# Non-local attention block: g projected by channels in two column halves and turned by transposes, second output projection one slot later

## The chip, the cores and the metric

One core of a Trainium2 chip runs the whole kernel. The metric is the device time of one execution in microseconds (us). Three executions of the kernel before took 215.80, 217.01 and 214.25 us, median 215.8. A fourth execution was profiled; it took 214.18 us.

## The reference

For each of 8 images, x is 128 channels by 1024 pixels (f32). Three 1x1 convolutions give theta and phi (64 channels each) and g (64 channels):

```
g     = w_g x + b_g          theta = w_theta x + b_theta      phi = w_phi x + b_phi
att   = softmax over m of (theta_n . phi_m)                   1024 x 1024 per image
y_n   = sum over m of att[n, m] g[m]
out   = x + BN(w_out y + b_out)                               BN: scale and shift by channel
```

The batch norm uses given means and variances, so it is one scale (INV) and one shift (SHIFT) by channel; the bias of g is folded into SHIFT.

## The kernel before

**Tiles.** An image has 8 tiles of 128 rows n of the attention matrix, the 8 images 64 tiles. Four tiles make a half (512 pixels), for which one value sum and one output projection are made. Every engine has its own program, written as a function `step(it, k)`; k counts tiles, and j = k % 8 is called the slot here. `run_steps` unrolls the first and last steps and puts 16 steps (two images) in a loop. The order within an engine is the order written out in `step`; between engines only semaphores order the work.

**A tile's way.** PE makes the scores of tile k+1 in step k (`scores`, L713: theta and phi split into high and low parts, four matmuls of 512 columns). VectorE takes the row maximum (L579), ScalarE the exponential with its row sum (L537), into `probs`. PE then turns the tile ("flips", L778, eight 128x128 transposes into the two banks ps_flip[0] and ps_flip[1]) in step k+2. ScalarE copies the flips as f16 high parts (pt_hi, L525), VectorE computes the f16 low parts (pt_lo, L678). One tile in four (slots 1 and 5) goes another way: GpSimd splits it (p_hi L402, p_lo L406) and the DMA queue transposes it (L296, L305), so steps 3 and 7 have no flips. A flip set may overwrite a bank of ps_flip only when pt_lo of the flip set before has read it (`pt_lo_ready`). The scores of tile k+1 overwrite the bank of tile k-1 and wait for its exponential (`probs_ready`).

**A half's way.** The value sums accumulate in ps_y: `sum_high` (L725, eight matmuls of f16, stationary 128 columns) in slots 3 and 7, `sum_low` (L732, eight matmuls of 64 stationary columns, alternating between the two column halves of the array) in slots 5 and 1. VectorE scales the sum into y_norm in slots 6 and 2 (`scale_y`, L596). PE makes the output projection into the bank ps_misc (`convolve`, L739) in the same slots 6 and 2. VectorE adds it to the residual (`add_residual`, L589) in slots 7 and 3, and SyncE's queue stores it.

**The next image.** PE also computes the projections of image b+1 while image b is worked on, all in the same bank ps_misc: theta/phi in slots 0 and 1 (L803), g in slot 4 (`project_g`, L697: for each of 8 pixel tiles x is the stationary operand and w_g moves, so that pixels come out on partitions). ScalarE copies g to g_raw in slot 5 (`evacuate_g`, L481). VectorE takes the peak of g in slot 6 (`peak_of_g`, L573), PE transposes it over all partitions in slot 7 (`spread_peak`, L719), and VectorE reads it in slot 0 and computes the scale (L647 to L656). GpSimd then makes the f16 parts of g: g_parts high and g_scaled in slot 0, g_parts low in slot 1 (L410 to L419). GpSimd also splits theta/phi (hi in slot 2, lo in slots 3 and 4) and x (x_hi, x_lo in slots 5 and 7), and writes the residual's start (resid, L448, slot 1). The high and low parts of theta/phi are restacked by six DMAs per image (L286); the scores of the next image's first tile, made in slot 7, wait for all of them (`stacked`).

**The DMA queue.** SyncE issues in one order per image (`image`, L327): inverse sums to DRAM, store of the second half of image b-2 (L283), x loads (L264, waiting for resid), transpose of p_hi, broadcast of inverse sums, transpose of p_lo, restacks of hi, store, inverse sums, restacks of lo, broadcast, transposes.

## Time and profile before

| | |
|---|---|
| median of three runs | 215.8 us (214.25 to 217.01) |
| the profiled execution's own time | 214.18 us |
| its span, first to last instruction | 212.4 us |
| PE busy | 202.0 us (95%) |
| VectorE (DVE) busy | 181.7 us (86%) |
| ScalarE (ACT) busy | 143.4 us (68%) |
| GpSimd (POOL) busy | 130.6 us (61%) |
| mean granted TensorE clock | 1.000 |
| share of PE in the chain that ended last | 61% |

The page gives one profiled execution. Busy shares say how full an engine is, not whether the end waits for it. The chain of waits goes back from the last instruction to what released each step; the timeline gives the start and length of each instruction in order, with the releaser of idle time in square brackets. In rows of PE, "x8" counts recorded matmuls; an f32 matmul that isn't a transpose is recorded as two. The span leaves out what lies around the instructions, here 1.8 us.

### The profile page before, as it was taken

What the parts mean: (1) busy time and instruction counts of PE and PEld (TensorE: products, weight loads), DVE (VectorE), ACT (ScalarE), POOL (GpSimd) and SP (SyncE); (2) the same over time, 40 slices, a digit from 0 to 9 for tenths busy, and PEclk for the clock granted to TensorE, in tenths of its full rate; (3) what the DMA queues carried; (4) which work ended last, traced back from release to release, by engine and by line L of the source; (5) the groups of instructions that cost most, each with busy time, mean ns of one, the idle gap of its engine ahead of it and who ended that gap; (6) DMA issues with size and microseconds to landing.
All of it is one profiled execution on the core that took longest, in us unless ns stands there. A gap on an engine that the chain in (4) does not pass through costs nothing.

```text
span 212.4 us, 4045 instructions
## 1 busy us (share of the span) xinstructions
PE 202.0 (95%) x1156; PEld 137.4 (65%) x1156; DVE 181.7 (86%) x298; ACT 143.4 (68%) x259; POOL 130.6 (61%) x113
## 2 busy tenths in 40 slices
PE   7997969999999999999999999999999999999994
PEld 6685838576665857577575956668575855656542
DVE  0689987987999799977999599977999789989871
ACT  2777857668585848866596666856696585758721
POOL 2449786848489494866679494885769352913400
PEclk9999999999999999999999999999999999999999
DMA  5225991699529974599819994299924994182102
GB/s 159 83 76 109 210 225 27 174 221 238 114 78 241 245 182 99 126 209 250 158 50 218 243 217 113 87 223 251 167 63 105 222 235 104 38 195 49 49 11 91
DMA packets 44716, 31.61 MB, mean 149 GB/s; under 512 B 35616, under 2 KB 36128, under 8 KB 44704
## 3 DMA queue, kind: packets, MB, share of 16 engines
q1 hardware_dynamic: 44416, 31.34, 63.7%
q10 hardware_dynamic: 288, 0.14, 0.2%
q8 instruction: 5, 0.08, 0.2%
q14 instruction: 7, 0.06, 0.1%
HBM read 8.36 MB, written 4.23 MB: 59 GB/s over the span
## 4 chain that ended last, share of the span: by engine, by line
PE 61%; DVE 14%; issue 8%; ACT 6%; DMA 4%; SPq 3%; POOL 2%; ACTq 1%; DVEq 0%
PE ps_scores L713 18%; PE ps_flip L778 13%; PE ps_y L725 10%; PE ps_misc L697 5%; DVE pt_lo L678 5%; PE ps_y L732 5%; DVE neg_max L579 5%; PE ps_misc L803 4%; PE ps_misc L739 4%; ACT probs L537 3%; DVE y_norm L596 2%; DMA phi_ll<-lo 2%; DMA vec<-vectors_dram 2%; SPq L286 2%; ACT pt_hi L525 2%
## 5 line engine op out<-in xcount | busy, mean ns | idle before, releaser
L537 ACT ACTIVATE probs<-ps_scores,neg_max 128x1024 f32<-128x1024 f32 x64 | 71.7, 1121 | 22.5 <-DVE neg_max L579 22.4
L579 DVE TENSOR_REDUCE neg_max<-ps_scores 128x1 f32<-128x1024 f32 x64 | 77.8, 1215 | 1.2 <-PE ps_scores L713 1.2
L678 DVE SCALAR_TENSOR_TENSOR pt_lo<-ps_flip,pt_hi 128x512 f16<-128x512 f32 x98 | 62.9, 684 | 15.3 <-ACT pt_hi L525 15.1
L525 ACT ACTIVATE pt_hi<-ps_flip 128x512 f16<-128x512 f32 x98 | 53.4, 597 | 26.5 <-PE ps_flip L778 26.5
L778 PE MATMUL ps_flip<-ident,probs 128*128 128x128 f32 x392 | 52.7, 276 | 1.1 <-DVE pt_lo L678 0.6
L778 PEld LDWEIGHTS ps_flip<-ident,probs 128*128 128x128 f32 x392 | 43.6, 142 | 13.8 <-issue 6.1
L713 PE MATMUL ps_scores<-phi_hh,theta_hl 128*128 128x512 f32 x128 | 45.7, 438 | 3.8 <-DMA phi_ll<-lo 1.8
L713 PE MATMUL ps_scores<-phi_ll,theta_hl 128*128 128x512 f32 x128 | 40.0, 393 | 0.0
L406 POOL TENSOR_TENSOR p_lo<-probs,p_hi 128x1024 f16<-128x1024 f32 x15 | 32.3, 2155 | 2.9 <-POOL p_hi L402 2.3
L725 PE MATMUL ps_y<-pt_hi,g_parts 128*128 128x512 f16 (+1 forms) x128 | 30.0, 377 | 0.0
L713 PEld LDWEIGHTS ps_scores<-phi_hh,theta_hl 128*128 128x128 f32 x128 | 19.3, 190 | 14.9 <-ACT probs L537 12.2
L713 PEld LDWEIGHTS ps_scores<-phi_ll,theta_hl 128*128 128x128 f32 x128 | 24.0, 188 | 5.6
L402 POOL TENSOR_SCALAR p_hi<-probs 128x1024 f16<-128x1024 f32 x15 | 15.7, 1047 | 10.8 <-ACT probs L537 9.8
L725 PEld LDWEIGHTS ps_y<-pt_hi,g_parts 128*128 128x128 f16 x128 | 11.4, 98 | 15.4 <-issue 4.2
L457 POOL TENSOR_SCALAR x_hi<-x_in 128x1024 fp32r<-128x1024 f32 x7 | 7.4, 1055 | 18.5 <-PE ps_misc L697 15.7
L462 POOL TENSOR_TENSOR x_lo<-x_in,x_hi 128x512 fp32r<-128x512 f32 x14 | 17.8, 1278 | 0.8
L432 POOL TENSOR_TENSOR lo<-qk,hi 128x512 fp32r<-128x512 f32 x14 | 17.8, 1294 | 0.8
L410 POOL TENSOR_SCALAR g_parts<-g_raw,g_factor 128x512 f16<-128x512 f32 x7 | 4.9, 694 | 20.5 <-DVE g_factor L654 20.5
L739 PE MATMUL ps_misc<-y_norm,wout 128*128 128x512 f32 x30 | 16.2, 621 | 0.9 <-DVE y_norm L596 0.9
L596 DVE SCALAR_TENSOR_TENSOR y_norm<-ps_y,y_unit,inv_all 128x512 f32<-128x512 f32 x15 | 17.0, 1135 | 0.0
L732 PE MATMUL ps_y<-pt_lo,g_parts 128*64 128x512 f16 (+1 forms) x128 | 16.7, 382 | 0.0
L697 PEld LDWEIGHTS ps_misc<-wg,x_in 128*128 128x128 f32 x112 | 13.6, 191 | 0.6
(80 smaller groups left out, 179.3 us busy)
## 6 DMA issues: line engine op xcount, KB each, us to landing
x_in<-x_in_dram SPq DMA_DIRECT2D x16, 256.0 KB, 3.2
inv_all<-inv_row SPq DMA_DIRECT2D x15, 256.0 KB, 3.7
out_dram<-resid SPq DMA_DIRECT2D x15, 256.0 KB, 3.1
phi_hh<-hi SPq DMA_DIRECT2D x14, 256.0 KB, 4.9
phi_ll<-lo SPq DMA_DIRECT2D x14, 256.0 KB, 4.1
theta_hl<-hi SPq DMA_DIRECT2D x7, 256.0 KB, 4.0
theta_hl<-lo SPq DMA_DIRECT2D x7, 256.0 KB, 3.8
pt_hi<-p_hi SPq DMA_TRANSPOSE x15, 3.6
```

What stands on the lines that cost most here:

```text
L406: nc.gpsimd.tensor_tensor(low[:, :], p[:, :], high[:, :], ALU.subtract).then_inc(p_lo_ready, 1)
L525: nc.scalar.activation(pt_hi[ring][:, c * HALF_TILES:(c + 1) * HALF_TILES, slot * P:(slot + 1) * P], ps_flip[c][:, :].rearrange("p (a n) - ...
L537: nc.scalar.activation(probs[k % PROB_RING][:, :], ps_scores[k % 2][:, :], ACT.Exp, bias=neg_max[:, k % STEPS:k % STEPS + 1], accum_out=ro ...
L579: nc.vector.tensor_reduce(out=top, in_=ps_scores[k % 2][:, :], op=ALU.max, axis=AX.X, negate=True).then_inc(row_max_ready if by_dma(it, k) ...
L596: nc.vector.scalar_tensor_tensor(out=y_norm[:, :].rearrange("c (t p) -> c t p", p=P), in0=ps_y[:, :].rearrange("c (t p) -> c t p", p=P), s ...
L678: nc.vector.scalar_tensor_tensor(out=pt_lo[ring][where], in0=ps_flip[c][:, :].rearrange("p (a n) -> p a n", n=P), scalar=PROB_SCALE, in1=p ...
L697: last = nc.tensor.matmul(target[:, m * CI:(m + 1) * CI], x_in[r][:, m * P:(m + 1) * P], wg[:, :], start=True, stop=True)
L713: last = nc.tensor.matmul(ps_scores[k % 2][:, cc], theta_hl[r][:, cols], phi[:, cc], start=(n == 0), stop=(n == 1))
L725: nc.tensor.matmul(target[:, to], g_parts[r][:, m, :], pt_hi[ring][:, m, cols], start=(m == 0), stop=False, skip_group_check=True)
L732: last = nc.tensor.matmul(target[side * CI:(side + 1) * CI, to], g_parts[r][:, m, 0:CI], pt_lo[ring][:, m, cols], start=False, stop=(m >= ...
L739: nc.tensor.matmul(target, wout[:, 0:C], y_norm[:, cols], start=True, stop=True).then_inc(conv_ready, 1)
L778: last = nc.tensor.transpose(ps_flip[c][:, a * P:(a + 1) * P], probs[(k - 2) % PROB_RING][:, m * P:(m + 1) * P], ident[:, :])
```

## The change

- PE, slot 5: g of the next image is computed with w_g (64 columns) as the stationary operand and x moving, 512 pixels for each of two f32 matmuls; pixels 0 to 511 go to partitions 0 to 63 of ps_misc, pixels 512 to 1023 to partitions 64 to 127. It stands directly behind `sum_low`. The eight matmul pairs of slot 4 are gone.
- ScalarE, slot 6: ps_misc is copied to the new buffer g_channels. PE, slot 6: four 128x128 transposes turn it back into ps_misc. ScalarE, slot 7: g_raw is copied from there, with its pixel tiles reordered.
- The peak of g is taken in slot 0 of the next image (VectorE), spread through ps_y in slot 2 (PE, after y_norm of that slot has been made), read in slot 3 (VectorE). The high-half sums of slot 3 wait for that read. GpSimd's three g_parts operations follow in slot 4. Both halves of lo are made in slot 3.
- The output projection of the second half goes from slot 6 to slot 7 (behind the high-half sums, waiting for the copy of g_raw), its residual addition from slot 7 to slot 0 of the next image. The theta/phi projection of slot 0 waits for that addition.
- x_hi waits for the theta/phi projections in place of the g projection.
- VectorE's program unrolls 16 first steps in place of 8.

```diff
--- before.py
+++ after.py
@@ -102,6 +102,7 @@
         theta_hl = [sbuf(f"theta_hl{i}", [P, N], F32R) for i in range(2)]
         phi_hh = [sbuf(f"phi_hh{i}", [P, N], F32R) for i in range(2)]
         phi_ll = [sbuf(f"phi_ll{i}", [P, N], F32R) for i in range(2)]
+        g_channels = sbuf("g_channels", [P, BANK], F32)
         g_raw = sbuf("g_raw", [P, MT, CI], F32)
         g_scaled = sbuf("g_scaled", [P, MT, CI], F32)
         g_parts = [sbuf(f"g_parts{i}", [P, MT, 2 * CI], F16) for i in range(2)]
@@ -163,6 +164,8 @@
         hi_ready = sem("hi_ready")
         lo_ready = sem("lo_ready")
         g_ready = sem("g_ready")
+        g_channels_out = sem("g_channels_out")
+        g_flipped = sem("g_flipped")
         g_out = sem("g_out")
         g_peak_ready = sem("g_peak_ready")
         g_peak_spread = sem("g_peak_spread")
@@ -405,7 +408,21 @@
                     hold(lo_moved[ring], moved_by(it, k - 1) - MOVED)
                     nc.gpsimd.tensor_tensor(low[:, :], p[:, :], high[:, :],
                                             ALU.subtract).then_inc(p_lo_ready, 1)
-                if j == 0 and exists(b, B) and not is_first(b):
+                if j == 2 and exists(b + 1, B):
+                    hold(proj_out, 2 * b + 2)
+                    if not is_first(b):
+
+                        hold(stacked[r], it * 16 * STACKS + 16 * STACKS * ((k // MT + 1) // 2))
+                    nc.gpsimd.tensor_scalar(out=hi[:, :], in0=qk[:, :], scalar1=1.0, scalar2=0.0,
+                                            op0=ALU.mult, op1=ALU.add).then_inc(hi_ready, 1)
+                if j == 3 and exists(b + 1, B):
+                    hold(hi_ready, b + 1)
+                    for c in range(PER_IMAGE):
+                        cols = slice(c * BANK, (c + 1) * BANK)
+                        nc.gpsimd.tensor_tensor(lo[:, cols], qk[:, cols], hi[:, cols].bitcast(F32),
+                                                ALU.subtract).then_inc(lo_ready, 1)
+
+                if j == 4 and exists(b, B) and not is_first(b):
                     hold(g_factor_ready, b + 1)
                     nc.gpsimd.tensor_scalar(out=g_parts[r][:, :, 0:CI], in0=g_raw[:, :, :],
                                             scalar1=g_factor[:, r:r + 1], scalar2=1.0,
@@ -413,27 +430,13 @@
                     nc.gpsimd.tensor_scalar(out=g_scaled[:, :, :], in0=g_raw[:, :, :],
                                             scalar1=g_factor[:, r:r + 1], scalar2=1.0,
                                             op0=ALU.mult, op1=ALU.mult).then_inc(g_scaled_ready, 1)
-                if j == 1 and exists(b, B) and not is_first(b):
                     hold(g_hi_ready, b + 1)
                     hold(g_scaled_ready, b)
                     nc.gpsimd.tensor_tensor(g_parts[r][:, :, CI:2 * CI], g_scaled[:, :, :],
                                             g_parts[r][:, :, 0:CI], ALU.subtract).then_inc(g_split, 1)
 
-                if j == 2 and exists(b + 1, B):
-                    hold(proj_out, 2 * b + 2)
-                    if not is_first(b):
-
-                        hold(stacked[r], it * 16 * STACKS + 16 * STACKS * ((k // MT + 1) // 2))
-                    nc.gpsimd.tensor_scalar(out=hi[:, :], in0=qk[:, :], scalar1=1.0, scalar2=0.0,
-                                            op0=ALU.mult, op1=ALU.add).then_inc(hi_ready, 1)
-                if j in (3, 4) and exists(b + 1, B):
-                    cols = slice((j - 3) * BANK, (j - 2) * BANK)
-                    hold(hi_ready, b + 1)
-                    nc.gpsimd.tensor_tensor(lo[:, cols], qk[:, cols], hi[:, cols].bitcast(F32),
-                                            ALU.subtract).then_inc(lo_ready, 1)
-
                 if j == 5 and exists(b + 2, B):
-                    hold(g_ready, b + 2)
+                    hold(proj_ready, 2 * b + 2)
                     split_x(it * 16 + 16 * (k // STEPS + 2), r, 0)
                     split_x(b + 2, r, 1)
                 if j == 7 and exists(b + 2, B):
@@ -511,9 +514,13 @@
                     nc.scalar.activation(qk[:, c * BANK:(c + 1) * BANK], ps_misc[:, :], ACT.Identity,
                                          bias=BIAS_TP).then_inc(proj_out, 1)
 
-                if j == 5 and exists(image + 1, B):
+                if j == 6 and exists(image + 1, B):
                     act.wait_ge(g_ready, image + 2)
-                    evacuate_g(image + 1, ps_misc[:, :], g_raw[:, :, :].rearrange("p t c -> p (t c)"))
+                    nc.scalar.activation(g_channels[:, :], ps_misc[:, :], ACT.Copy).then_inc(g_channels_out, 1)
+                if j == 7 and exists(image + 1, B):
+                    act.wait_ge(g_flipped, image + 1)
+                    evacuate_g(image + 1, ps_misc[:, :].rearrange("p (a c i) -> p a c i", c=PER_IMAGE, i=CI),
+                               g_raw[:, :, :].rearrange("p (c a) i -> p a c i", c=PER_IMAGE))
 
                 t = tile_at(it, k - 2)
                 if exists(t, TILES) and not by_dma(it, k - 2):
@@ -630,21 +637,15 @@
                 if tile_is(it, k, TILES + 1):
                     scale_y(HALVES - 2, 0, 1, B - 1, 8 * HALVES)
 
-                h = half_at(it, k - 11)
-                if j % HALF_TILES == 3 and exists(h, HALVES - 2):
-                    ring, part = (k - 11) // MT % 2, (k - 11) // HALF_TILES % PER_IMAGE
-                    dve.wait_ge(resid_ready, image_at(it, k - 11) + 1)
-                    add_residual(h, resid[ring][:, part * BANK:(part + 1) * BANK], ps_misc[:, :])
                 if tile_is(it, k, 1):
                     peak_of_g(0, 0)
-                if j == 6 and exists(image + 1, B):
-                    peak_of_g(image + 1, (k // MT + 1) % 2)
-
-                if j == (2 if is_first(image) else 0) and exists(image, B):
+                if j == 0 and exists(image, B) and not is_first(image):
+                    peak_of_g(image, k // MT % 2)
+
+                if j == (2 if is_first(image) else 3) and exists(image, B):
                     r = k // MT % 2
                     dve.wait_ge(g_peak_spread, image + 1)
-                    spread = ps_y if is_first(image) else ps_misc
-                    nc.vector.tensor_reduce(out=g_peak_all[:, r:r + 1], in_=spread[:, 0:P], op=ALU.max,
+                    nc.vector.tensor_reduce(out=g_peak_all[:, r:r + 1], in_=ps_y[:, 0:P], op=ALU.max,
                                             axis=AX.X).then_inc(g_peak_read, 1)
                     dve.wait_ge(g_peak_read, image + 1)
                     nc.vector.tensor_scalar(out=g_unit[:, r:r + 1], in0=g_peak_all[:, r:r + 1],
@@ -656,6 +657,13 @@
                     nc.vector.tensor_scalar(out=y_unit[:, r:r + 1], in0=g_unit[:, r:r + 1],
                                             scalar1=1.0 / PROB_SCALE, scalar2=None,
                                             op0=ALU.mult).then_inc(y_unit_ready, 1)
+
+                back = 11 if j == 3 else 12
+                h = half_at(it, k - back)
+                if j in (0, 3) and exists(h, HALVES - 2):
+                    ring, part = (k - back) // MT % 2, (k - back) // HALF_TILES % PER_IMAGE
+                    dve.wait_ge(resid_ready, image_at(it, k - back) + 1)
+                    add_residual(h, resid[ring][:, part * BANK:(part + 1) * BANK], ps_misc[:, :])
 
                 if tile_is(it, k, 2):
                     dve.wait_ge(g_factor_ready, 1)
@@ -683,7 +691,7 @@
                 if exists(t, TILES):
                     row_maximum(it, k + 1)
 
-            run_steps(dve, step)
+            run_steps(dve, step, head=STEPS)
             dve.wait_ge(resid_ready, B)
             add_residual(HALVES - 2, resid[1][:, 0:BANK], ps_misc[:, :])
             add_residual(HALVES - 1, resid[1][:, BANK:N - P], ps_scores[1][:, 0:BANK - P])
@@ -793,8 +801,7 @@
                         if isinstance(image, int) and image == 0:
                             pe.wait_ge(w_lo_ready, 1)
                         pe.wait_ge(x_lo_ready, 2 * image + 1)
-                        if not is_first(image):
-                            pe.wait_ge(g_peak_read, image + 1)
+                        wait(pe, result_ready, 2 * image - 2)
                     else:
                         pe.wait_ge(x_lo_ready, 2 * image + 2)
                         pe.wait_ge(proj_out, 2 * image + 1)
@@ -804,18 +811,22 @@
                                                 start=(n == 0), stop=(n == 2))
                     last.then_inc(proj_ready, 1)
                 h = half_at(it, k - 10)
-                if j % HALF_TILES == 2 and exists(h, HALVES - 2):
+                if j == 2 and exists(image, B) and not is_first(image):
+                    pe.wait_ge(y_scaled, 2 * image - 1)
+                    spread_peak(image, k // MT % 2, ps_y[:, 0:P])
+                if j == 2 and exists(h, HALVES - 2):
                     if more:
-                        pe.wait_ge(*((proj_out, 2 * image + 2) if j == 2 else (g_out, image + 2)))
+                        pe.wait_ge(proj_out, 2 * image + 2)
                     else:
                         wait(pe, result_ready, h)
                     convolve(h, ps_misc[:, :], slice(0, BANK))
 
-                if j == 4 and more:
-                    pe.wait_ge(proj_out, 2 * image + 2)
-                    wait(pe, result_ready, 2 * image - 1)
-                    project_g(ps_misc, (k // MT + 1) % 2, range(MT)).then_inc(g_ready, 1)
-
+                if j == 6 and more:
+                    pe.wait_ge(g_channels_out, image + 1)
+                    for a in range(HALF_TILES):
+                        last = nc.tensor.transpose(ps_misc[:, a * P:(a + 1) * P],
+                                                   g_channels[:, a * P:(a + 1) * P], ident[:, :])
+                    last.then_inc(g_flipped, 1)
 
                 h, quarter = half_at(it, k - 6), (k - 6) % HALF_TILES
                 if exists(h, HALVES - 2):
@@ -825,6 +836,8 @@
                         pe.wait_ge(hi_moved[ring], moved_by(it, k - 6))
                         pe.wait_ge(g_split, image_at(it, k - 6) + 1)
                         wait(pe, y_scaled, h)
+                        if j == 3:
+                            pe.wait_ge(g_peak_read, image_at(it, k) + 1)
                         sum_high(ring, r, ps_y, slice(0, BANK), slice(0, BANK))
                     if quarter == 3:
                         pe.wait_ge(lo_moved[ring], moved_by(it, k - 6))
@@ -832,9 +845,22 @@
 
                 if tile_is(it, k, 1):
                     spread_peak(0, 0, ps_y[:, 0:P])
-                if j == 7 and more:
-                    wait(pe, result_ready, 2 * image)
-                    spread_peak(image + 1, (k // MT + 1) % 2, ps_misc[:, 0:P])
+                if j == 5 and more:
+                    pe.wait_ge(proj_out, 2 * image + 2)
+                    wait(pe, result_ready, 2 * image - 1)
+                    for c in range(PER_IMAGE):
+                        last = nc.tensor.matmul(ps_misc[c * CI:(c + 1) * CI, :], wg[:, :],
+                                                x_in[(k // MT + 1) % 2][:, c * BANK:(c + 1) * BANK],
+                                                start=True, stop=True, skip_group_check=True)
+                    last.then_inc(g_ready, 1)
+
+                h = half_at(it, k - 11)
+                if j == 7 and exists(h, HALVES - 2):
+                    if more:
+                        pe.wait_ge(g_out, image + 2)
+                    else:
+                        wait(pe, result_ready, h)
+                    convolve(h, ps_misc[:, :], slice(0, BANK))
 
                 if tile_is(it, k, TILES - 1):
                     pe.wait_ge(pt_lo_ready, 2 * flip_at(0, LAST_HALF))
```

## Rows read from the trace of the kernel before

**Rows 1.** The page's first part, busy time of each engine.

```profile
PE 202.0 (95%) x1156; PEld 137.4 (65%) x1156; DVE 181.7 (86%) x298; ACT 143.4 (68%) x259; POOL 130.6 (61%) x113
```

**Rows 2.** Windows view, images 1 to 5: length, then busy us of PE, PEld, DVE, ACT, POOL.

```profile
34.36:155.65 121.29, 120.60 (x697) 82.23 (x696) 109.15 (x176) 85.30 (x156) 84.72 (x70) 1.00 0.74 171
```

**Rows 3.** The chain of waits, in image 2: start us, us, engine and tile.

```profile
61.71 0.98 PE ps_y L732 x8
...
64.65 0.86 PE ps_misc L739 x2
...
66.73 1.74 PE ps_y L725 x8
```

**Rows 4.** Timeline of all engines, PE's rows: start us, us, engine, line, operation.

```profile
141.46 1.04 PE L778 MATMUL ps_flip<-ident,probs 128*128 128x128 f32 x8
...
143.26 1.89 PE L697 MATMUL ps_misc<-wg,x_in 128*128 128x64 f32 x16
...
144.99 1.04 PE L778 MATMUL ps_flip<-ident,probs 128*128 128x128 f32 x8
...
146.89 1.05 PE L732 MATMUL ps_y<-pt_lo,g_parts 128*64 128x512 f16 x8
...
147.87 1.09 PE L778 MATMUL ps_flip<-ident,probs 128*128 128x128 f32 x8
...
149.90 1.13 PE L739 MATMUL ps_misc<-y_norm,wout 128*128 128x512 f32 x2
...
150.80 0.73 PE L713 MATMUL ps_scores<-phi_hh,theta_hl 128*128 128x512 f32 x2
...
151.84 1.90 PE L725 MATMUL ps_y<-pt_hi,g_parts 128*128 128x512 f16 x8
...
153.69 1.04 PE L778 MATMUL ps_flip<-ident,probs 128*128 128x128 f32 x8
```

**Rows 5.** The same timeline, three rows of ACT.

```profile
145.27 0.60 ACT L481 ACTIVATE g_raw<-ps_misc 128x512 f32<-128x512 f32 x1 [0.99 <-PE ps_misc L697]
...
148.57 1.09 ACT L525 ACTIVATE pt_hi<-ps_flip 128x512 f16<-128x512 f32 x2 [0.62 <-PE ps_flip L778]
...
149.54 1.12 ACT L537 ACTIVATE probs<-ps_scores,neg_max 128x1024 f32<-128x1024 f32 x1
```

**Rows 6.** Timelines of PE and DVE in the last image.

```profile
189.35 1.04 PE L778 MATMUL ps_flip<-ident,probs 128*128 128x128 f32 x8
...
191.46 1.16 PE L778 MATMUL ps_flip<-ident,probs 128*128 128x128 f32 x8
...
193.48 1.05 PE L732 MATMUL ps_y<-pt_lo,g_parts 128*64 128x512 f16 x8
...
190.62 1.29 DVE L678 SCALAR_TENSOR_TENSOR pt_lo<-ps_flip,pt_hi 128x512 f16<-128x512 f32 x2 [0.81 <-ACT pt_hi L525]
```

**Rows 7.** Timeline of all engines, four rows of DVE.

```profile
146.39 1.29 DVE L678 SCALAR_TENSOR_TENSOR pt_lo<-ps_flip,pt_hi 128x512 f16<-128x512 f32 x2 [1.05 <-ACT pt_hi L525]
...
149.77 0.68 DVE L573 TENSOR_REDUCE g_peak<-g_raw 128x1 f32<-128x512 f32 x1
...
152.69 0.74 DVE L589 SCALAR_TENSOR_TENSOR resid<-ps_misc,bn,resid 128x512 f32<-128x512 f32 x1
...
154.75 0.28 DVE L647 TENSOR_REDUCE g_peak_all<-ps_misc 128x1 f32<-128x128 f32 x1
```

**Rows 8.** Timelines of PE and DVE, slot 3 of the last image.

```profile
187.62 1.90 PE L725 MATMUL ps_y<-pt_hi,g_parts 128*128 128x512 f16 x8
...
187.67 0.74 DVE L589 SCALAR_TENSOR_TENSOR resid<-ps_misc,bn,resid 128x512 f32<-128x512 f32 x1
```

**Rows 9.** Timeline of PE, slot 6 of the last image.

```profile
196.69 1.10 PE L739 MATMUL ps_misc<-y_norm,wout 128*128 128x512 f32 x2 [0.20 <-DVE y_norm L596]
```

**Rows 10.** Timeline of the DMA queue: restacks of the low parts.

```profile
145.54 1.30 SPq L286 DMA_DIRECT2D phi_ll<-lo  x2
```

**Rows 11.** The page's DMA issues: count, KB each, median us to landing.

```profile
phi_ll<-lo SPq DMA_DIRECT2D x14, 256.0 KB, 4.1
```

## The prediction, made before the changed kernel was run

> **What bounds the kernel now.** I read the page's engine line first [rows 1]: PE is busy 95% of the span, VectorE 86%, so PE is the candidate and VectorE is close behind. A share over the whole span says nothing about a stage, so I read next the five whole images from the first to the sixth theta/phi projection [rows 2]: 121.29 us, or 24.26 us per image, with PE busy 120.60 of them and VectorE 109.15. The chain of waits then says whether PE's busy time is really what the end waits for. In these images it is mostly PE work in sequence, and its pieces give the prices without queueing [rows 3]: the value matmuls on the low halves ("low-half sums") 0.98 us, an output projection 0.86, the high-half sums 1.74. The g projection costs 1.73 by its start and the next one's [rows 4].
>
> Last, the timeline of one image, because order is what changes. I call the start of the probability flips of slot n F(n), and the start of the scores issued in slot 7 S. The rows [rows 4] give F(2) 141.46, g projection 143.26, F(3) 144.99, low-half sums 146.89, F(4) 147.87, output projection 149.90, S 150.80, high-half sums 151.84, F(6) 153.69. From F(4) to S are 2.93 us, and PE alone doesn't need them. The scores at S overwrite a bank that the exponential of tile 6 must have read; that exponential stands behind two pt_hi copies, which start 0.70 us after F(4), and itself starts 0.97 us after them [rows 5]. From there to S are 1.26 us. So the output projection at 149.90 lies in a shadow: without it S would come at 150.80 all the same. Everywhere else between F(2) and the next F(6) PE is the chain.
>
> **The change, part by part.**
>
> (a) The old g projection leaves slot 4. It stood between F(2) and the low-half sums, which are 146.89 - 141.46 = 5.43 us apart. The last image has no g projection in slot 4 and the same work otherwise: 193.48 - 189.35 = 4.13 us [rows 6]. That is a gain of 1.30 us, not of 1.74: with nothing between slot 4's scores and F(3), the flips of tile 3 must wait until VectorE has read the halves of tile 2's flips out of the two flip banks. In that image pt_lo begins 1.27 us after F(2) and F(3) follows 2.11 us after F(2) [rows 6]. What is late next after the removal is therefore VectorE's pt_lo.
>
> (b) The new g projection, two f32 matmuls of 512 columns into the two column halves, comes behind the low-half sums and in front of F(4), hence on the path. No row shows f32 matmuls in column halves. The bounds: one f32 output projection of 512 columns costs 0.86 [rows 3], so two side by side cost 0.86 and two in sequence 1.72. The nearest row is the low-half group: eight f16 matmuls in column halves 0.98 against eight of full width 1.74, so neighbours in different halves do run beside each other. But an f32 matmul is two passes (the output projection is recorded as x2). In program order they are half 0 first pass, half 0 second pass, half 1 first, half 1 second; only the middle two are neighbours in different halves. Three times 0.43 is 1.28 us, which I take.
>
> The Trainium skill, "TensorE: Matmul & The Clock Gate", Part 3, gives a packed group the span of one matmul plus a few ns for each further tile. By that model the pair would cost about 0.86; the f16 group agrees with it, and nothing here shows f32.
>
> (c) The four transposes in slot 6, half a flip set, so about 0.4 us, take the projection's place in the shadow from F(4) to S: 0.85 for flips, 1.0 for scores, 0.4 are 2.3 of 2.93 us. Cost nothing; were the shadow gone, 0.4. Before them ScalarE copies g_channels, one more 128x512 copy per image. It takes the place that the g copy had, in front of the pt_hi copies and during the first flips, so I cost it at nothing; with that cover gone it is at most the 0.60 of the g copy [rows 5]. The copy back from the transposes moves to slot 7, where ScalarE waits for a row maximum.
>
> (d) The second output projection moves out of the shadow into slot 7, behind the high-half sums and in front of F(6), on the path: +0.86. The peak transpose that stood there goes to slot 2, into the same kind of shadow: its place was 0.11 [from rows 4, 151.84 + 1.74 to 153.69]. Net +0.75.
>
> (e) VectorE. The g peak, 0.68 us, leaves slot 6, where this engine is latest, and the residual addition, 0.74, leaves slot 7; both go to slot 0 of the next image, and the read of the spread peak, 0.28 and three shorter ones, leaves it for slot 3 [rows 7]. Slot 0 grows by between 0.25 and 1.1, I take 0.6. In exchange slots 6 and 7 are never late any more. The image of rows 4 took 24.02, the mean is 24.26; I credit the difference, 0.24, between zero and that. PE newly waits at the first theta/phi projection for that residual addition. After the projection in slot 7 PE issues a flip set and scores, 1.8 us, first; the addition can begin some 1.1 after the projection's start and lasts 0.74, so it is just in time. The wait of slot 3's high-half sums on the peak's read is met within 0.1 in these images, by the same counting.
>
> (f) GpSimd and the DMA queue. The three g_parts operations go from slots 0 and 1 to slot 4, between lo and x_hi, where it used to idle; their reader is in slot 7. The store of the second half is queued behind a residual that comes later, ahead of the x loads and p_hi's transpose in the DMA queue; but it was already held by the inverse sums in front of it, so it slips only some 0.3. The last restack of phi_ll is issued at about 146.2 and lands 4.1 later, at 150.3, against 150.80 for S [rows 10, 11]: 0.5 us of slack, which this 0.3 eats, while S itself comes later. Nothing, or up to 0.3 per image.
>
> The sum for one of images 1 to 6: -1.30 + 1.28 + 0.75 - 0.24 = +0.49, in six images +2.9. In image 0 the g projection lies beside the wait for the first restacks: 0. In the last image VectorE is the chain: the maximum of tile 3 ends at 187.67, where the residual addition begins, and the high-half sums start at 187.62 [rows 8]. With 0.28 of peak read in front of them and slot 0's 0.6, that is +0.9. At the tail the projection at 196.69 waits for y_norm, and a flip set stands behind it [rows 9]; with the order turned, these flips fill the wait in part, but they wait for pt_lo, and the projection no longer hides: between -0.5 and +0.9, I take +0.4. **Total +4.2 us.** The profiled execution took 214.18, its span is 212.4; the median of the runs shown is 215.8, 1.6 higher. I put the base between them, 215.0: 219.2, that is 2.0% more.
>
> **Rivals.**
>
> *The column halves really pair in f32* (b = 0.86): per image +0.07, in all +1.7, 216.7. For it speaks the f16 group; against it that an f32 matmul's two passes use the same half in succession. Chance 0.22.
>
> *They don't overlap at all* (b = 1.74, about two output projections in sequence): per image +0.95, in all +7.0, 222.0. For it: f32 passes already take twice the time per column, so reading the columns may be what limits, and two streams would share it. Chance 0.20.
>
> *VectorE is the true bound, so the result is faster.* VectorE runs without a gap from slot 5 of one image to slot 4 of the next. One of its gaps is 1.05 us before pt_lo of tile 3, at 146.39 [rows 7], and the g projection in front of F(3) makes it. If this engine sets the period, the gap closes and the images get 1.05 shorter: -6.3 + 1.3 for the ends = -5.0, 210.0. It decides if PE has a microsecond to give in slot 7 for the moved output projection. Against it: PE is busy 120.60 of 121.29 us, and the chain runs over PE there. Chance 0.12.
>
> *The order of PE is not what I think* (a restack that lands late, or the ends worse): 0.04. My own case has 0.42.
>
> **Numbers.** This kernel can tell about 2% from no change, 4.3 us. My case lies at that line, half on each side (0.21 and 0.21). Slower: 0.21 + 0.19 of the case without overlap + 0.02 = 0.42. Faster: 0.10, nearly all of the VectorE case. Within 2%: 0.48. The range goes from 213.0 to 222.5: it holds the three cases with g at 0.86, 1.28 and 1.74 with their unknown ends, and reaches part of the way to the VectorE case; the likeliest case alone would be 218.0 to 220.5.
>
> **What would show it.** In the profile after: the time from F(2) to the low-half sums near 4.1; the time from the end of the low-half sums to F(4) is (b) directly, 1.28 or one of the two rivals; F(4) to S still 2.9; S to F(6) 3.6; pt_lo as the releaser of F(3). I am wrong if S to F(6) stays at 2.9, if F(4) to S shrinks, or if VectorE has no gap left in slots 4 to 6.

## The result, and the profile after

The changed kernel takes 218.88 us (median of 4, 218.44 to 219.84) against 216.4; the ratio is 1.0157 (95% interval 1.0091 to 1.0222). Ratios and intervals leave out executions more than 1.5% above their kernel's fastest, and they are not the quotients of the medians given beside them (here 1.0115). Forecast were 219.2 us and 2.0% more. The profiled execution took 218.50 us. Its span is 216.3 us, 3.9 more than the span of the profiled execution before, 212.4, where the working had 4.2. The total is near, but several of its terms are not, and they cancel.

The windows view of the same five images (length, busy us of PE, PEld, DVE, ACT, POOL), to set beside [rows 2]:

```profile
35.08:158.54 123.46, 119.54 (x657) 77.25 (x655) 111.96 (x176) 88.60 (x161) 83.97 (x69) 1.00 0.73 168
```

24.69 us per image, +0.43. PE is busy 1.1 us less and the images last 2.2 us longer, so PE now waits: 3.9 us in place of 0.7. The timeline of one image, PE's rows (start, us), beside [rows 4]. F(2) is 144.20, F(3) 146.22, F(4) 150.18, S 153.10 and F(6) 156.74:

```profile
144.20 1.04 PE L786 MATMUL ps_flip<-ident,probs 128*128 128x128 f32 x8
...
146.22 1.25 PE L786 MATMUL ps_flip<-ident,probs 128*128 128x128 f32 x8
...
148.33 1.05 PE L740 MATMUL ps_y<-pt_lo,g_parts 128*64 128x512 f16 x8
149.22 1.02 PE L852 MATMUL ps_misc<-x_in,wg 128*64 128x512 f32 x4
150.18 1.09 PE L786 MATMUL ps_flip<-ident,probs 128*128 128x128 f32 x8
...
152.04 0.60 PE L827 MATMUL ps_misc<-ident,g_channels 128*128 128x128 f32 x4
153.10 0.73 PE L721 MATMUL ps_scores<-phi_hh,theta_hl 128*128 128x512 f32 x2 [0.47 <-ACT probs L544]
...
154.14 1.90 PE L733 MATMUL ps_y<-pt_hi,g_parts 128*128 128x512 f16 x8
155.88 1.02 PE L747 MATMUL ps_misc<-y_norm,wout 128*128 128x512 f32 x2
156.74 0.49 PE L786 MATMUL ps_flip<-ident,probs 128*128 128x128 f32 x3
```

And VectorE's row beside [rows 6]: the half of tile 2's flips is read from 145.47, 1.27 us after F(2), and F(3) follows 2.02 us after F(2).

```profile
145.47 1.29 DVE L686 SCALAR_TENSOR_TENSOR pt_lo<-ps_flip,pt_hi 128x512 f16<-128x512 f32 x2 [0.64 <-ACT pt_hi L532]
```

What changed in each segment, as means of images 1 to 5 in each trace (F(n) is the start of the flips of slot n and S that of the scores of slot 7, as in the prediction):

| segment | before | after | change | forecast |
|---|---|---|---|---|
| F(2) to low-half sums | 5.43 | 4.13 | -1.30 | -1.30 |
| low-half sums to F(4) | 0.98 | 1.85 | +0.86 | +1.28 |
| F(4) to S | 2.98 | 3.20 | +0.21 | 0 to +0.3 |
| S to F(6) | 3.03 | 3.63 | +0.60 | +0.75, less 0.24 of VectorE's lateness |
| F(6) to F(2) | 11.83 | 11.89 | +0.06 | 0 |
| one image | 24.26 | 24.69 | +0.43 | +0.49 |

In three of these five images the scores of slot 7 come late, 3.46, 3.51 and 3.13 us after F(4), and their rows name a releaser, the restack of phi_ll, that none of images 1 to 6 had in the trace before:

```profile
54.61 0.72 PE L721 MATMUL ps_scores<-phi_hh,theta_hl 128*128 128x512 f32 x2 [1.00 <-DMA phi_ll<-lo]
...
104.05 0.73 PE L721 MATMUL ps_scores<-phi_hh,theta_hl 128*128 128x512 f32 x2 [1.06 <-DMA phi_ll<-lo]
```

The parts of the 3.9 us, by the starts of F(6) in image 0 (32.40 before, 33.27 after) and in image 6 (177.89 and 181.16): 0.9 us are added in front of the first, 2.4 in the six images between, 0.6 behind the second. Of the 0.9, 0.5 lie before image 0's first split theta/phi projection (12.63 and 13.16), in a part that the change doesn't touch; the other traces have it anywhere from 12.44 to 13.19. The rest goes with the restack of image 0, whose scores of slot 7 start at 30.50 in place of 29.52. The last image's high-half sums of slot 3 now wait for the peak's read, beside [rows 8], and at the tail the flips stand in front of the projection and wait themselves, beside [rows 9]:

```profile
191.06 1.89 PE L733 MATMUL ps_y<-pt_hi,g_parts 128*128 128x512 f16 x8 [0.49 <-DVE g_peak_all L648]
...
200.73 1.16 PE L786 MATMUL ps_flip<-ident,probs 128*128 128x128 f32 x8 [0.81 <-DVE pt_lo L686]
201.73 1.02 PE L747 MATMUL ps_misc<-y_norm,wout 128*128 128x512 f32 x2
```

### The profile page after: what moved, and what is told of

Read it like the earlier page. It is cut to its first block, busy times and chain, and to the rows that moved or that the text cites. A ratio compares the mean times of both kernels' runs of the same rounds, so it can differ in the third digit from the quotient of the medians.

```text
span 216.3 us, 3894 instructions
## 1 busy us (share of the span) xinstructions
PE 201.2 (93%) x1100; PEld 130.8 (60%) x1100; DVE 184.7 (85%) x298; ACT 148.2 (69%) x266; POOL 130.0 (60%) x113
## 4 chain that ended last, share of the span: by engine, by line
PE 45%; DVE 13%; SPq 10%; issue 10%; DMA 8%; ACT 6%; POOL 6%; POOLq 0%; ACTq 0%; DVEq 0%
PE ps_scores L721 12%; PE ps_y L733 10%; PE ps_flip L786 9%; DMA phi_ll<-lo 6%; DVE pt_lo L686 5%; SPq L289 5%; DVE neg_max L586 4%; PE ps_misc L747 4%; ACT probs L544 4%; PE ps_y L740 3%; POOL p_lo L409 3%; PE ps_scores L759 2%; PE ps_misc L810 2%; POOL p_hi L405 2%; SPq L318 2%
## 5 line engine op out<-in xcount | busy, mean ns | idle before, releaser
L532 ACT ACTIVATE pt_hi<-ps_flip 128x512 f16<-128x512 f32 x98 | 54.0, 595 | 36.8 <-PE ps_flip L786 36.8
L786 PE MATMUL ps_flip<-ident,probs 128*128 128x128 f32 x392 | 53.6, 278 | 2.3 <-DVE pt_lo L686 1.7
L451 POOL TENSOR_SCALAR resid<-x_in,bn 128x1024 f32<-128x1024 f32 x8 | 9.0, 1122 | 35.6 <-DMA out_dram<-resid 34.4
L747 PE MATMUL ps_misc<-y_norm,wout 128*128 128x512 f32 x30 | 15.4, 596 | 0.5 <-DVE y_norm L603 0.5
L596 DVE SCALAR_TENSOR_TENSOR resid<-ps_misc,bn,resid 128x512 f32<-128x512 f32 x15 | 11.2, 747 | 3.3 <-PE ps_misc L747 3.0
L544 ACT ACTIVATION_READ_ACCUMULATOR probs<-ps_scores,neg_max 128x1 f32 x64 | 13.1, 205 | 0.0
```

The costliest lines, as they stand in the source:

```text
L532: nc.scalar.activation(pt_hi[ring][:, c * HALF_TILES:(c + 1) * HALF_TILES, slot * P:(slot + 1) * P], ps_flip[c][:, :].rearrange("p (a n) - ...
L544: nc.scalar.activation(probs[k % PROB_RING][:, :], ps_scores[k % 2][:, :], ACT.Exp, bias=neg_max[:, k % STEPS:k % STEPS + 1], accum_out=ro ...
L747: nc.tensor.matmul(target, wout[:, 0:C], y_norm[:, cols], start=True, stop=True).then_inc(conv_ready, 1)
L786: last = nc.tensor.transpose(ps_flip[c][:, a * P:(a + 1) * P], probs[(k - 2) % PROB_RING][:, m * P:(m + 1) * P], ident[:, :])
```

## The experiments

**1. The moved work with the old g** (`e2_old_g_new_order`): the two halves of the change taken apart. The four transposes of slot 6 and the two f32 matmuls of slot 5 go, the old g projection stands in slot 4 again.

```diff
-                if j == 6 and more:
...
+                if j == 4 and more:
...
+                    project_g(ps_misc, (k // MT + 1) % 2, range(MT)).then_inc(g_ready, 1)
...
-                if j == 5 and more:
```

> The changed kernel's order (second output projection in slot 7, its addition in slot 0, peak read in slot 3, g_parts in slot 4) with the old g projection: eight matmul pairs by pixels in slot 4, copied to g_raw in slot 5, no transposes. Theory A (PE's order is the path): F(2) to the low-half sums goes back from 4.12 to 5.43 us, the low-half sums to F(4) from 1.85 to 0.98, together +0.44 per image, 2.6 us in six images; since S comes later, the restack waits (1.3 us in images 1 to 6) shrink. Whole: 1 to 2.6 us longer than the changed kernel, 219.9 to 221.5. Rival B (the new g brings nothing, its transposes and extra copy cost what it saves): same or shorter than the changed kernel, 218 to 219.

221.97 us, ratio 1.0239 (1.0146 to 1.0332). F(2) to the low-half sums is 5.43, these to F(4) 0.98, as before; S to F(6) is 3.62 to 3.64 in every image. So the moved output projection and the rest of the new order cost about 2.4%, and the new g gives about 0.8% back. The rival falls: images 1 to 5 take 124.83 us, 1.37 more than in the changed kernel. The whole says it less cleanly than the images. Of the 3.9 us between the two spans (220.2 and 216.3) 2.1 lie before image 1's first theta/phi projection, where PE waits 2.88 us for the first restacks and the granted clock then falls (see the last section). Five of six images show no restack wait: S is later here.

**2. Both g matmuls in one column half** (`e3_same_half`). Half of g is left out.

```diff
-                        last = nc.tensor.matmul(ps_misc[c * CI:(c + 1) * CI, :], wg[:, :],
+                        last = nc.tensor.matmul(ps_misc[0:CI, :], wg[:, :],
```

> The changed kernel with both f32 matmuls of the new g projection written to the same column half (partitions 0 to 63), so half of g is left out of the result. Theory A (0.87 us for the pair because matmuls in different column halves run side by side in f32 too): the time from the low-half sums to F(4) rises from 1.85 to about 2.7 us, the whole by 6 x 0.86 less the restack waits, +3.5 to +5 us, 222 to 224. Rival B (a 64-column f32 matmul is cheap by itself, or its two passes overlap): 1.85 us stays and so does the whole.

One execution, 221.74 us. Timeline of PE:

```profile
124.64 1.05 PE L740 MATMUL ps_y<-pt_lo,g_parts 128*64 128x512 f16 x8
125.53 1.88 PE L852 MATMUL ps_misc<-x_in,wg 128*64 128x512 f32 x4
127.34 1.09 PE L786 MATMUL ps_flip<-ident,probs 128*128 128x128 f32 x8
```

2.70 us from the low-half sums to F(4), 0.85 more than with two halves: f32 matmuls in different halves run side by side, and my count of three passes in sequence was wrong. All six images show 2.92 or 2.93 us from F(4) to S: with S 0.86 us later, no restack is late. An image takes 25.28 us on average, only 0.58 more than after, because 0.27 of restack wait is gone.

**3. The restacks issued first** (`e1_restack_first`, and `e5_before_restack_first` on the kernel before).

```diff
-                store(it, k - MT)
-                inv_to_row(2 * b)
                 if exists(b + 1, B):
                     sp.wait_ge(lo_ready, 2 * b + 2)
...
                     restack(phi_ll[1 - r], CI, lo, CI, 1 - r)
+                store(it, k - MT)
+                inv_to_row(2 * b)
```

> The changed kernel with one difference in the DMA queue's order: the three restacks of the low parts of theta/phi are issued ahead of the store of the first half and ahead of the inverse-sum row, which stand in front of them in the changed kernel (about 2.3 us of issue time). Theory A: in the changed kernel the scores of slot 7 wait in four of seven images for the last restack of phi_ll to land (from F(4) to S 3.46, 3.51 and 3.13 us in place of 2.93; image 0 has 1.7 us of wait). With the restacks 2 us earlier all of images 1 to 6 show 2.92 to 2.96 us from F(4) to S, image 0's wait is 0 to 0.7 us, and the whole is 1.5 to 2.5 us shorter than the changed kernel: 216.4 to 217.4. Rival B: these waits come from ScalarE, which has one more copy per image in front of the exponential of tile 6; then the time from F(4) to S and the whole stay (218.5 to 219).

> The kernel before, with the restacks of the low parts issued ahead of the store of the first half and of the inverse-sum row. Theory A: in the kernel before only image 0 waits for a restack (2.2 us at 29.5); F(4) to S falls there from 3.9 to about 2.9 us, nothing changes elsewhere: 1.0 us shorter than before, 0.995 of it. Rival B (the queue's order also sets something in the other images, for example the inverse sums or the x loads): a change of 2 us or more in either direction.

217.71 us, ratio 1.0076 (1.0036 to 1.0116): 1.2 us less than the changed kernel by the medians, where 1.5 to 2.5 were expected, and the two intervals overlap. On the kernel before 0.9978 (0.9936 to 1.0019), no difference that can be told. Image 0's wait, which was to shrink in both, did not: 1.88 us where the changed kernel has 1.72, and 1.75 where the kernel before has 1.81. In the changed kernel with this order images 1 to 6 show 2.92, 2.93, 3.04, 2.92, 3.68, 3.08. The waits of images 1 and 3 shrink to 0 and 0.1 us, but one of 0.75 comes in image 5. The page's DMA issues give a likely reason why little is won; the row of the changed kernel, then the row of this one:

```profile
phi_ll<-lo SPq DMA_DIRECT2D x14, 256.0 KB, 4.2
```

```profile
phi_ll<-lo SPq DMA_DIRECT2D x14, 256.0 KB, 5.7
```

Issued closer together, each takes 1.5 us longer to land (5.6 in place of 4.1 on the kernel before). The rows of the late scores name the restack. How much of the pattern by image comes from the order is not shown: the trace of experiment 8's `e13_after_fill`, with the queue's code unchanged, has 3.60, 2.98, 4.14, 3.36, 3.96 and 2.93 us in the same six places, so the waits differ widely from one trace to the next.

**4. Less traffic** (`e10_small_stores`): whether the DMA engines are full. Most of the result is left out.

```diff
-                sp.dma_start(dst, resid[ring][:, cols]).then_inc(stored[ring], 16)
+                sp.dma_start(dst[:, 0:64], resid[ring][:, part * BANK:part * BANK + 64]).then_inc(stored[ring], 16)
```

> The changed kernel with every store of a half (but the last pieces) cut to 64 of its 512 columns, so most of the result is left out. Nothing on the engines changes, the DMA engines carry some 0.45 MB less per image. Theory A (the restacks land late because the DMA engines are full, not because the queue issues late; issuing them earlier in e1 made each take 5.3 us instead of 4.3): the waits of the slot-7 scores for phi_ll go in images 1 to 6 (F(4) to S 2.92 to 3.0 everywhere), and the images take 24.4 us each instead of 24.7 on average; 1.0 to 1.5 us less in all. Rival B (the order and issue times in the queue decide): the waits of 0.2 to 0.6 us stay.

217.69 us in one execution. F(4) to S: 3.33, 2.93, 3.66, 2.92, 2.93, 2.93. Images 2, 4, 5 and 6 are free of waits, images 1 and 3 are not, and phi_ll still takes 4.3 us to land. Neither theory holds whole: with most of the stores' bytes gone, images 1 and 3 are still late. The trace of the changed kernel shows two ways to be late. In image 3 the second restack of phi_ll is issued at 99.75, 0.79 us before F(4); in images 1, 2, 4 and 5 it is 1.4 to 1.8 us before. In image 1 it is issued at 49.3, early enough, but the scores that wait for it start only at 54.61; the longest of the 14 restacks took 5.2 us to land, the median 4.2. Why these two images differ stays open, and with one trace of each kernel it can't be told how much of it is chance.

**5. The new g in slot 4** (`e4_g_in_slot_4`).

```diff
-                if j == 6 and exists(image + 1, B):
+                if j == 5 and exists(image + 1, B):
                     act.wait_ge(g_ready, image + 2)
...
+                if j == 4 and more:
+                    pe.wait_ge(proj_out, 2 * image + 2)
...
-                if j == 5 and more:
-                    pe.wait_ge(proj_out, 2 * image + 2)
```

> The changed kernel with the new g projection in slot 4, between the scores of slot 4 and F(3), in place of slot 5 behind the low-half sums; its copy by ScalarE in slot 5, the transposes stay in slot 6. Theory A (F(3) waits for pt_lo of tile 2 when nothing stands in front of it): the g projection fills that wait, F(2) to F(4) falls from 5.97 to about 5.6 us; but S then waits longer for the restacks, so the whole is only 0 to 1.5 us shorter than the changed kernel: 217.4 to 219. Rival B (being directly behind the other matmuls in column halves is what makes the new g cheap, through a change of mode of the array): F(2) to F(4) rises to over 6.1 us and the whole by 1 us or more, 220.

221.22 us, ratio 1.0221 (1.0130 to 1.0312); slower than the changed kernel by the medians, though the two intervals overlap. F(2) to F(4) is 5.84 us: 0.13 less than after, where 0.37 was expected. Timeline of PE:

```profile
146.75 1.04 PE L786 MATMUL ps_flip<-ident,probs 128*128 128x128 f32 x8
147.55 0.71 PE L721 MATMUL ps_scores<-phi_hh,theta_hl 128*128 128x512 f32 x2
...
148.65 1.08 PE L828 MATMUL ps_misc<-x_in,wg 128*64 128x512 f32 x4
149.66 1.09 PE L786 MATMUL ps_flip<-ident,probs 128*128 128x128 f32 x8
```

The group costs 1.01 us to the next start, and the scores in front of it take 1.10, where the old g projection, at full width, follows scores after 1.01 [from rows 4, F(2) to the g projection 1.80 with 0.79 of flips]. Behind the low-half sums the same group adds 0.87. So going into column halves and out again seems to cost some 0.2 us, which the place behind the low-half sums saves; no run tests another reason for the difference. The Trainium skill, "TensorEngine Tiling (Array Packing)", Key Properties, says that a change of tiling mode drains the engine; these rows fit that, with 0.2 us for both changes, but don't show a drain as such. What is left of the gain is then lost to the restacks: F(4) to S is 3.61, 3.00, 4.07, 3.18, 3.16, 2.92, so images 1 to 5 take 123.77 us against 123.46. Nearly all of the extra time of this trace lies before them: image 1's first theta/phi projection starts 2.3 us later than in the changed kernel, of 2.5 us between the spans. PE waits longer for image 0's restacks there, and then runs at a lower clock for a while:

```profile
31.14 0.73 PE L721 MATMUL ps_scores<-phi_hh,theta_hl 128*128 128x512 f32 x2 [3.52 <-DMA phi_ll<-lo]
...
32.18 3.55 PE L733 MATMUL ps_y<-pt_hi,g_parts 128*128 128x512 f16 x8
```

So the whole doesn't measure the place of g; the two segments do.

**6. Transposes made twice** (`e7_transposes_twice`).

```diff
-                    for a in range(HALF_TILES):
+                    for a in (0, 1, 2, 3) * 2:
```

> The changed kernel with the four transposes of slot 6 made twice over. Theory A (they lie in the shadow from F(4) to S, in which PE has 2.93 - 0.85 - 1.0 - 0.45 = 0.6 us left): F(4) to S stays at 2.92 in the images without restack wait, and the whole stays within 0.5 us. Rival B (they are on the path): +0.45 us per image, +2.7 us.

219.62 us in one execution. Images 4 to 6 show 3.04, 3.11 and 2.92 from F(4) to S, the first three 3.83, 3.62, 3.93. The image at 2.92 has 0.43 us more of transposes and no more time, so they do lie in the shadow. In the first three PE waits 0.94, 0.73 and 1.03 us for the restack of phi_ll after the transposes are issued, so it is the restack that sets S there. Whether the transposes have a part in its coming later than in the changed kernel (by 0.37, 0.66 and 0.42 us) is not shown. The whole, 0.7 us more than the changed kernel's median, says nothing by itself.

**7. The new g with the output projection left in slot 6** (`e8_slots_4_5_6`; with the restacks first `e9_slots_4_5_6_restack_first`).

```diff
-                    project_g(ps_misc, (k // MT + 1) % 2, range(MT)).then_inc(g_ready, 1)
+                    for c in range(PER_IMAGE):
+                        last = nc.tensor.matmul(ps_misc[c * CI:(c + 1) * CI, :], wg[:, :],
...
+                if j == 5 and more:
+                    pe.wait_ge(g_channels_out, image + 1)
+                    for a in range(HALF_TILES):
```

The two f32 matmuls stand in slot 4, in place of the old projection; ScalarE copies them in slot 5, the four transposes stand in slot 5 behind the scores, and ScalarE copies g_raw in slot 6.

> The kernel before with the new g projection, but its second output projection left in slot 6: g by channels in slot 4, copied by ScalarE in slot 5, four transposes in slot 5 behind the scores, g_raw copied in slot 6, peak in slot 6 and read in slot 0 as before. Theory A (PE's order is the path; the moved output projection is what costs): F(2) to the low-half sums 5.0 to 5.2 us instead of 5.43, everything else as before, so 0.25 to 0.45 per image shorter than the kernel before, 1.5 to 2.7 us, if VectorE's lateness in slot 6 does not eat it: ratio 0.988 to 0.997. Rival B (VectorE is the bound in slots 6 and 7): no gain, since VectorE only waits in slots 4 and 5; ratio 1.00.

> The same as e8_slots_4_5_6 with the restacks of the low parts issued first. Theory A: what e8 and e5 gain adds up, since the restacks are then nowhere late: 1.0 us (image 0) plus any restack wait that the shorter images of e8 show. Ratio to the kernel before 0.98 to 0.992. Rival B: no more than e8.

215.09 us, ratio 0.9917 (0.9869 to 0.9965): 0.8% faster than the kernel before. With the restacks first 216.23, 0.9978 (0.9911 to 1.0045): nothing more, where the two gains were to add up; image 0's wait is 2.75 us there. Timeline of PE:

```profile
119.50 1.04 PE L785 MATMUL ps_flip<-ident,probs 128*128 128x128 f32 x8
...
121.39 1.08 PE L825 MATMUL ps_misc<-x_in,wg 128*64 128x512 f32 x4
122.40 1.09 PE L785 MATMUL ps_flip<-ident,probs 128*128 128x128 f32 x8
...
124.27 0.60 PE L833 MATMUL ps_misc<-ident,g_channels 128*128 128x128 f32 x4
124.79 1.05 PE L739 MATMUL ps_y<-pt_lo,g_parts 128*64 128x512 f16 x8
125.78 1.09 PE L785 MATMUL ps_flip<-ident,probs 128*128 128x128 f32 x8
...
127.64 1.03 PE L746 MATMUL ps_misc<-y_norm,wout 128*128 128x512 f32 x2
```

F(2) to the low-half sums is 5.30, 0.13 less than before, S to F(6) 2.88 in every image. The projection is in the shadow again, and VectorE's lateness between S and F(6) is gone. But restack waits take most of that back: F(4) to S is 3.85, 2.93, 3.42, 2.97, 3.29 and 2.92 us, and images 1 to 5 take 121.09 us in this trace against 121.29 before. The part from image 6's first theta/phi projection to the end is 0.9 us shorter (56.1 against 56.9), the start is longer (36.55 against 34.20). So the gain that is left in this trace lies mostly behind image 5.

**8. PE kept busy in the first wait** (`e11_slots_4_5_6_fill`, `e12_before_fill`, `e13_after_fill`).

```diff
+                if tile_is(it, k, MT - 1):
+                    for _ in range(8):
+                        nc.tensor.matmul(ps_y[:, 0:P], warm[:, :], warm[:, :], start=True, stop=True)
```

> e8_slots_4_5_6 with eight matmuls of zeros into ps_y put in front of the slot-7 scores of image 0, where PE waits for the first restacks. Theory A: in the traces in which that wait was 2.9 us or more the granted clock fell to half for a part of the next windows (0.83 as a mean over 10 us), and the next image took 0.8 to 1.7 us longer; where it was 1.8 us it stayed at 1.00. The eight matmuls take 0.9 to 1.8 us of the wait and cost nothing; the clock stays 1.00 in every execution, and the median falls from 215.1 to about 213.8 us, ratio to the kernel before 0.982 to 0.99. Rival B (the clock falls for another reason): it falls in some executions all the same, ratio 0.99 to 0.995.

> The kernel before with the same eight matmuls of zeros. Theory A: its executions spread over 214.3 to 218.8 us because the clock falls in a part of them; with the matmuls they lie within 1 us of 214.3 us, ratio 0.99. Rival B: the same spread, ratio 1.00.

> The changed kernel with the same eight matmuls of zeros. Theory A: 218.3 us with a small spread; against e12_before_fill it shows the change's own price without the clock's part: 3.5 to 4.5 us, the sum of +0.43 us for each of five images, 0.7 for the first and about 1 for the last two. Rival B: 218.9 us as before, with the same spread.

e8's order with the fill: 213.2 us (213.03 to 213.59), ratio 0.9821 (0.9734 to 0.9909), the best version found. Of e8's own ten executions eight had a mean granted clock of 0.992 or less; the other two took 213.59 and 214.09 us. The kernel before with it: 216.04 (215.07 to 217.37), ratio 1.0046 (1.0011 to 1.0082), so no gain, and my expectation for it was wrong. The changed kernel with it: 218.48 (217.96 to 219.93), 1.0097 (1.0055 to 1.0138). Against e12 that is 2.4 us for the change, less than the 3.5 to 4.5 expected; no execution of one (217.96 and more) reaches those of the other (217.37 and less). The ratios, only 0.5% apart, would put it lower still. In the trace of e12 restack waits of 0.33 and 0.37 us stand in images 2 and 3, where the kernel before has none; whether the fill makes them is not shown. The windows of e8 and then of e11, from 28 to 38 us (the granted clock is the third number from the end):

```profile
28.00:33.00 5.00, 2.76 (x7) 1.50 (x8) 2.92 (x4) 1.96 (x4) 2.77 (x2) 0.73 1.08 213
33.00:38.00 5.00, 5.00 (x31) 3.67 (x30) 3.40 (x10) 2.62 (x5) 2.12 (x3) 0.93 0.02 2
```

```profile
28.00:33.00 5.00, 4.23 (x26) 2.77 (x25) 3.36 (x6) 1.66 (x4) 2.48 (x2) 1.00 0.86 195
33.00:38.00 5.00, 5.00 (x31) 4.09 (x29) 4.02 (x10) 4.43 (x8) 3.63 (x4) 1.00 0.02 4
```

## Why the prediction was right, and where its steps were not

- **The number.** 219.2 us forecast, 218.88 measured: in part luck. The base was taken as 215.0, the record has 216.4, 1.4 us more; the medians then differ by 2.5 us, where the working had 4.2. Between the two traces it is 3.9, but the trace before is of one of its kernel's fastest executions (214.18 us, where 56 others have 214.09 at the least). The 3.9 are 2.4 in six images for 2.9, 0.9 at the start for 0, 0.6 in the last image and the tail for 1.3.
- **(a) right.** -1.30 as forecast, with pt_lo as the next late one. The neighbouring image without a g projection gave the price that the duration of the removed group (1.73) would have missed.
- **(b) wrong, a term mis-sized.** 1.28 forecast, 0.87 measured; experiment 2 shows that it is the halves that do it. The first rival's condition came true. The span that "TensorE: Matmul & The Clock Gate", Part 3 of the Trainium skill, gives a packed group, one matmul's, agrees with the 0.87 (one f32 projection: 0.86). But that rival's time, 216.7, didn't come: 2.5 us too much in six images for (b) were made up by the restack waits of (f), a little by (e), and by the start.
- **(f) under-priced.** I gave the restacks 0.5 us of slack and a slip of at most 0.3. With g cheaper, S wants to come about 0.4 us earlier, and the slack is gone: in five images 1.3 us of wait (0.27 per image beyond 2.93). Experiments 1 and 2 show it from the other side: where S is later by other work, the waits go, but for one of 0.5 us. The size is that of one trace; in the trace of `e13_after_fill` the waits come to 3.4 us in six images.
- **(d) right.** S to F(6) is 3.63; 2.9 + 0.75 were forecast. It is the term that decides the sign, and experiments 1 and 7 show it: old g in the new order is slower than the kernel before by 2.4%, new g in the old order faster by 0.8%.
- **(c) right** as far as tested: no time in the image of experiment 6 that has no restack wait.
- **(e) near in sum.** VectorE's lateness before is gone: S to F(6) was 3.29 and 3.19 us in two of five images and 2.89 in the others, and F(4) to S 3.22 in one. That is 1.0 us in five images, 0.20 each, where 0.24 was credited. New is 0.06 in F(6) to F(2), where the high-half sums of slot 3 now wait for the peak's read.
- **The ends.** 1.3 forecast, 1.5 between the two traces: 0.9 at the start, where I had nothing, and 0.6 in the last image and the tail, where I had 0.9 + 0.4. That the sums come near each other is chance.
- **The VectorE rival fails**: between F(2) and pt_lo VectorE still idles (0.64 us), and the changed kernel is slower, not 5 us faster.

## What to carry to other kernels

Before moving an instruction out of a place that looks full, ask what it lies beside: this projection was free in the shadow of an exponential and cost 0.75 us per image elsewhere. When one stage gets shorter, work out what arrives next from another engine or a DMA, and price the slack that the saving uses up. And undo the parts of a change one at a time: its good half, kept alone, beat both kernels. Compare traces by segments, too: the start of the kernel alone, with its one long wait, moved spans by over 2 us.

## What the runs showed of the hardware

- Two f32 matmuls of 512 columns with 64 stationary columns each cost 0.87 us in different column halves and 1.72 in the same one, behind other matmuls in column halves.
- The granted TensorE clock fell to half, 1.2 GHz, for a stretch after the first restack wait in some executions. In the traces of e8, e2, e4 and e1 PE had waited 2.44, 2.88, 3.52 and 1.88 us with nothing to do, and the windows from 28 to 38 us show 0.73 to 0.93; in e1 and e4 the high-half sums then took 3.54 and 3.55 us in place of 1.90. In e9 PE had waited 2.75 us and the same windows show 1.00, as they do behind 1.72 and 1.81 us in the changed kernel and the kernel before, and with the fill. So the length of this wait doesn't tell by itself whether the clock falls, and the expectation of experiment 8, by which waits of 1.8 us leave it up, doesn't hold as a rule. PE's rows of e1, then of e9:

```profile
30.14 0.73 PE L721 MATMUL ps_scores<-phi_hh,theta_hl 128*128 128x512 f32 x2 [1.88 <-DMA phi_ll<-lo]
...
31.17 3.54 PE L733 MATMUL ps_y<-pt_hi,g_parts 128*128 128x512 f16 x8
```

```profile
30.14 0.74 PE L720 MATMUL ps_scores<-phi_hh,theta_hl 128*128 128x512 f32 x2 [2.75 <-DMA phi_ll<-lo]
...
31.20 1.90 PE L732 MATMUL ps_y<-pt_hi,g_parts 128*128 128x512 f16 x8
```

- Of 56 executions of the kernel before, 29 had a mean clock of 0.997 or more and a median of 215.4 us, 27 had less and 217.5 us. All 24 executions with the fill had 0.997 or more, but it did not make the kernel before faster than its executions at full clock (216.04 against 215.4); why is open.
- Restacks of phi_ll, 256 KB each, landed a median of 4.1 to 4.6 us after their issue in the kernels with the queue's old order, and 5.5 to 5.7 us in the three kernels that issue the six restacks with no other DMA between.
